# Four graph layers on one core: the self edge taken out of the gather lists, its row loaded plainly, nine chunks of edges per tile instead of ten

## What is computed

```python
# layer 0: 4 heads, slope 0.2
Wh = h @ W ; e = leaky_relu(s_i[:, None] + s_j[None, :]) ; mask by adj ; alpha = softmax(e)
out = elu(alpha @ Wh)
# layer 1: 1 head, slope 0.01:   out = h @ W + softmax(e) @ h
# layer 2: 4 heads, slope 0.2, biases: out = softmax(e) @ (h @ W + b)
# layer 3: 4 heads: q, k, v = h @ Wq + bq, ... ; out = softmax(q k^T / 8 + mask) @ v
```

## Time and profile before

| | |
|---|---|
| median of 3 runs | 2135.06 us (2132.64 to 2135.48) |
| profiled execution, its own time | 2136.06 us |
| its span, first to last instruction | 2134.3 us |
| busy: PE / DVE / ACT / POOL | 1360.3 / 1511.9 / 828.1 / 1288.1 us |
| mean granted TensorE clock | 0.851 |
| gathers | 1280 indirect DMAs on POOL |

### The profile page before, as it was taken

One profiled execution on the slowest core, in us unless ns is written; L12 is line 12 of the kernel. 1 busy time (PEld: TensorE's weight loads), 2 busy tenths in 40 slices (PEclk: granted clock), 3 DMA queues, 4 the chain that ended last, 5 costly groups with the idle time before them and its releaser, 6 DMA issues.

```text
span 2134.3 us, 24746 instructions
## 1 busy us (share of the span) xinstructions
PE 1360.3 (64%) x8038; PEld 1000.1 (47%) x8038; DVE 1511.9 (71%) x3362; ACT 828.1 (39%) x1804; POOL 1288.1 (60%) x1300
## 2 busy tenths in 40 slices
PE   3565322777667526666677447777778567777775
PEld 2434221555555414454455235555555355555554
DVE  2768897888777635555557357777777389999997
ACT  5777352677655501222222102322223223333332
POOL 0000067777777167777776277777773477777771
PEclk9999999778777858877878668998989689888998
DMA  9998134444444134444444244454543577777772
GB/s 357 387 382 304 14 81 117 112 124 115 117 117 118 35 102 107 113 114 112 115 115 104 61 106 129 138 140 136 140 139 98 162 225 228 228 226 226 226 225 63
DMA packets 151094, 328.57 MB, mean 154 GB/s; under 512 B 31275, under 2 KB 62897, under 8 KB 150961
## 3 DMA queue, kind: packets, MB, share of 16 engines
q0 software_dynamic: 71680, 213.24, 36.9%
q1 hardware_dynamic: 61584, 92.57, 12.3%
q10 hardware_dynamic: 17696, 21.12, 2.9%
HBM read 294.93 MB, written 31.90 MB: 153 GB/s over the span
## 4 chain that ended last, share of the span: by engine, by line
POOL 56%; issue 20%; PE 7%; DVE 7%; ACT 5%; DMA 3%; SPq 1%; ACTq 0%; POOLq 0%; DVEq 0%
POOL s_gb L785 56%; PE ps L1814 3%; PE ps L1736 3%; ACT s_a L816 2%; DMA s_adj<-in_adj_dram 2%; DMA s_gb<-s_tab,s_ji 1%; DVE s_gb L1537 1%; DVE s_F L1473 1%; DVE s_F L1471 1%; SPq L634 1%; ACT s_tb L934 1%; DVE s_ST L1359 0%; ACT s_hb L857 0%; DMA s_tab<-s_tb 0%; ACT s_S L971 0%
## 5 line engine op out<-in xcount | busy, mean ns | idle before, releaser
L785 POOL DMA_INDIRECT s_gb<-s_tab,s_ji x1280 | 1283.7, 1003 | 551.8 <-issue 388.1
L1814 PE MATMUL ps<-s_gb,s_S 128*128 128x260 f32 (+1 forms) x2048 | 574.9, 443 | 28.5 <-DVE s_gb L1537 25.2
L1814 PEld LDWEIGHTS ps<-s_gb,s_S 128*128 128x128 f32 x2048 | 453.3, 227 | 117.7 <-DVE s_gb L1537 29.9
L1537 DVE TENSOR_TENSOR s_gb<-s_gb,ps 128x1024 f32<-128x1024 f32 (+1 forms) x288 | 284.8, 1031 | 0.1
L1736 PE MATMUL ps<-s_wx,s_hT 128*128 128x264 f32 (+2 forms) x512 | 221.8, 569 | 86.9 <-ACT s_tb L932 48.4
L1787 PE MATMUL ps<-s_ident,s_sc 128*16 128x128 f32 (+3 forms) x408 | 78.4, 347 | 289.5 <-DVE s_sc L1432 284.3
L1427 DVE TENSOR_TENSOR s_sc<-s_sc,s_gb 128x80 f32<-128x80 f32 (+3 forms) x51 | 11.5, 226 | 287.9 <-DMA s_gb<-s_tab,s_ji 286.2
L971 ACT ACTIVATE s_S<-s_count,s_ji 128x128 f32<-128x128 f32 x512 | 156.5, 397 | 145.6 <-PE ps L1814 129.7
L1787 PEld LDWEIGHTS ps<-s_ident,s_sc 128*16 128x16 f32 (+3 forms) x408 | 39.3, 104 | 313.5 <-DVE s_sc L1432 292.9
L1776 PE MATMUL ps<-s_qs,s_ST 128*128 128x256 bf16 x960 | 153.5, 329 | 45.5 <-DVE s_tmp L1454 31.0
L1736 PEld LDWEIGHTS ps<-s_wx,s_hT 128*128 128x128 f32 x512 | 111.6, 241 | 147.8 <-ACT s_tb L932 55.2
(11 more groups left out here) (201 smaller groups left out, 2026.7 us busy)
## 6 DMA issues: line engine op xcount, KB each, us to landing
s_adj<-in_adj_dram SPq DMA_DIRECT2D x32, 2048.0 KB, 17.0
s_gb<-s_tab,s_ji POOLq DMA_INDIRECT x1280, 3.2
s_tab<-s_tb ACTq DMA_DIRECT2D x32, 256.0 KB, 4.1
s_tab<-s_tb ACTq DMA_DIRECT2D x31, 260.0 KB, 3.9
s_qs<-s_q SPq DMA_DIRECT2D x32, 192.0 KB, 3.9
s_q<-s_qs SPq DMA_DIRECT2D x15, 384.0 KB, 2.9
...
```

Source lines behind the costliest of these rows:

```text
L785: e.indirect_dma_start(gb[:, 0, k, :], None, self.tab_d[L.n], bass.IndirectOffsetOnAxis(ap=self.idx[:, t, k:k + 1], axis=0)).then_inc(self ...
L1537: e.tensor_tensor(vv[:, k0:k1], vv[:, k0:k1], wide(p[:, k0:k1, :], 3, L.hd), ALU.mult).then_inc(self.weighed)
L1814: m = e.matmul(o, S[:, i, :], g4[:, 0, k, lo:lo + o.shape[1]], start=(k == 0), stop=(k == KT - 1))
```

## The change

The edge of a node to itself is taken out of the lists, so that nine chunks hold the edges of a tile. The node's own row comes by a plain load, 128 rows at a time, into `mine`. The own edge's score `z` is worked out per node when the table is made (`vec_si` for layers 0 to 2, `vec_z` for layer 3), spread over the edges with the target's score, enters the maximum, and its weight goes through the sum as extra columns; `vec_finish` adds own weight times own row. Besides, the subtraction of the maximum moves: `vec_shift` ends with the backward scan, PE turns the maxima back, and DVE subtracts them from the scores in four small instructions (`vec_less`), before which ACT's exponential can't start. Layer 1 multiplies its rows as the others do. In `vec_step`, `vec_less` stands behind the second finish, in `vec_last_step` at the end.

```diff
-KT = 10
+KT = 9
@@ sp_own, called for tiles 0 to 3 at a layer's start, then for the tiles of group n+2 at the end of step n @@
+    def sp_own(self, e, L, t):
+        g = T * L.n + t
+        if g >= 4:
+            e.wait_ge(self.evac, g - 3)
+        a = D if L.n == 3 else 0
+        self.sp_dma(e, self.mine[:, t % 4, :], self.tab_d[L.n][P * t:P * t + P, a:a + D], self.own_in[t % 4])
@@ gp_layer @@
             if L.n == 3:
                 e.wait_ge(self.q_proj, T)
+                e.wait_ge(self.zed, 17)
@@ act_exp @@
+        e.wait_ge(self.lessened, G + 1)
...
+        e.activation(self.p_bank(L, n), sc[:, :, :, 0:H], ACT.Exp).then_inc(self.p_ok)
+        for t in tiles:
+            m = e.activation(self.rows(L, t)[:, 0, :, self.pcols(L, 2)], sc[:, :, t - tiles[0], :], ACT.Exp)
@@ vec_si @@
+        e.tensor_tensor(z, tb[:, :, D:D + H], tb[:, :, D + H:D + 2 * H], ALU.add).then_inc(self.v)
+        e.wait_ge(self.v, vs.up())
+        e.scalar_tensor_tensor(z, z, L.slope, z, ALU.mult, ALU.max).then_inc(self.v)
@@ vec_z, called by vec_r before its own instruction @@
+        e.tensor_tensor(prod, self.bank(0, D * a, D * c).rearrange("p (j d) -> p j d", d=D), k, ALU.mult).then_inc(self.zed)
+        e.wait_ge(self.zed, m + 1)
+        e.tensor_reduce(z, prod.rearrange("p j (h d) -> p j h d", h=4), AX, ALU.add).then_inc(self.v)
+        e.wait_ge(self.v, vs.up())
+        e.tensor_scalar(z, z, 0.125, None, ALU.mult).then_inc(self.v)
+        e.wait_ge(self.v, vs.up())
+        self.vec_split(e, z, r, [self.si3[:, t0:t0 + c, n, 0:4] for n in range(3)], self.si_ok)   # 4 small instructions
@@ vec_scores (now in layer 3 too, in place of act_double) @@
+            e.scalar_tensor_tensor(flat, flat, L.slope, flat, ALU.mult, ALU.max).then_inc(self.v)
...
-            m = e.scalar_tensor_tensor(twice[:, :, s, :], raw[:, 4 * s:4 * s + HC, :], L.slope,
-                                       raw[:, 4 * s:4 * s + HC, :], ALU.mult, ALU.max)
+            m = e.tensor_tensor(twice[:, :, s], raw[:, 3 * s:3 * s + HC], z[:, 3 * s:3 * s + HC], ALU.max)
         m.then_inc(self.raw_ok)
+        e.tensor_tensor(z, z, first, ALU.add).then_inc(self.v)
@@ vec_shift @@
-        e.tensor_tensor(F, pc, F, ALU.subtract).then_inc(self.shifted)
+    def vec_less(self, e, L, n):
+        e.wait_ge(self.back, G + 1)
+        e.wait_ge(self.v, vs.n)
+        for a in (0, H):
+            for s, k0, k1 in ((0, 0, 5), (1, 5, KT)):
+                to = sc[:, k0:k1, :, a:a + H]
+                m = e.tensor_tensor(to, to, pt[:, k0 - 3 * s:k1 - 3 * s, s], ALU.subtract)
+        m.then_inc(self.lessened)
@@ vec_weigh: three products of three chunks a tile, in layer 1 too @@
+            k = slice(3 * u, 3 * u + 3)
+            if L.n in (1, 2):
                 self.vec_onehot(e, L, 3 * (T * L.n + t) + u)
+            e.tensor_tensor(vv[:, k], vv[:, k], wide(p[:, k, :], 3, L.hd), ALU.mult).then_inc(self.weighed)
@@ vec_finish @@
-        e.reciprocal(rc, op).then_inc(self.v)
+        e.tensor_scalar(q, oq, self.alone[:, t:t + 1], None, ALU.add).then_inc(self.v)
+        e.wait_ge(self.v, vs.up())
+        e.tensor_tensor(rc, op, q, ALU.add).then_inc(self.v)
+        e.wait_ge(self.own_in[t % 4], 16 * (8 * L.n + t // 4 + 1))
+        e.tensor_tensor(by_head(mine), by_head(mine), wide(q, 2, L.hd), ALU.mult).then_inc(self.v)
+        e.reciprocal(rc, rc).then_inc(self.v)
+        e.tensor_tensor(ov, ov, mine, ALU.add).then_inc(self.v)
@@ vec_last_step @@
         self.vec_spread(e, L, n)
         self.vec_dots(e, 2 * n + 3)
+        self.vec_scores(e, L, n + 1)
         self.vec_finish(e, L, 2 * n)
         self.vec_finish(e, L, 2 * n + 1)
         self.vec_shift(e, L, n + 1)
         self.vec_dots(e, 2 * n + 4)
+        self.vec_less(e, L, n + 1)
```

More of the change, by code:

```diff
@@ L475, in __init__ @@
         self.turned_raw, self.shifted, self.back, self.p_ok = sem("traw"), sem("shifted"), sem("back"), sem("p")
-        self.ones_ok, self.weighed, self.apart, self.S_ok, self.agg = (sem(n) for n in ("one", "wei", "apart", "S", "agg"))
+        self.lessened, self.weighed, self.apart, self.S_ok, self.agg = (sem(n) for n in ("less", "wei", "apart", "S", "agg"))
         self.evac, self.x_new, self.ex_in, self.ex_out = sem("evac"), sem("x_new"), sem("ex_in"), sem("ex_out")
         self.missed_ok, self.met_sum, self.sym_ok, self.sym = sem("missed"), sem("met"), sem("sym_ok"), sem("sym")
-        self.ruler = sem("ruler")
+        self.ruler, self.zed, self.own_in = sem("ruler"), sem("zed"), [sem(f"own{n}") for n in range(4)]
         self.out = sem("out")
@@ L561, in rows @@
     def rows(self, L, t, n=1):
-        size = KT * L.row
+        size = KT * L.slot
         at = (0 if L.n == 3 else LOW) + t % L.ring * size
@@ L716, in sp_layer @@
                     self.sp_q_load(e, t)
+            for m in {0: (14, 15), 1: (15, 16), 2: (15, 16), 3: (30, 31)}[L.n]:
+                e.wait_ge(self.tab_out[m % 2], self.stored(L.n, m))
+            for t in range(4):
+                self.sp_own(e, L, t)
         for n in range(lo, hi):
@@ L726, in sp_layer @@
                 self.sp_q_store(e, n - 2)
+            for t in self.tiles(n + 2) if n < 15 else ():
+                self.sp_own(e, L, t)
         if hi == 17:
@@ L914, in act_rows @@
                     e.wait_ge(self.tab_out[t % 2], self.stored(3, t - 2))
+                    e.wait_ge(self.zed, self.group(t - 2) + 1)
                 else:
@@ L961, in act_onehot @@
         g = T * L.n + t
[L962 to L964 removed]
+        if g == 0:
             e.wait_ge(self.listed, 8)
@@ L968, in act_onehot @@
         for U in range(3 * g, 3 * g + 3):
-            many, k0 = self.many(U)
-            for i in range(many):
-                m = e.activation(self.s_part(U)[:, i, :], self.count[:], ACT.Square,
-                                 bias=self.irel[:, t, k0 + i:k0 + i + 1], scale=-1.0)
+            for i in range(3):
+                k = 3 * (U % 3) + i
+                m = e.activation(self.s_part(U)[:, i, :], self.count[:], ACT.Square, bias=self.irel[:, t, k:k + 1], scale=-1.0)
             m.then_inc(self.apart)
@@ L1169, in vec_norm, with vec_split @@
                                ALU.mult).then_inc(self.normed)
[L1171 to L1179 removed]
+    def vec_split(self, e, src, r, si, last):
+        vs = self.vs
         e.tensor_copy(si[0], src).then_inc(self.v)
@@ L1185, in vec_si @@
         e.wait_ge(self.v, vs.up())
+        e.tensor_tensor(si[2], r, si[1], ALU.subtract).then_inc(last)
+    def vec_si(self, e, l, m):
+        L, vs = LAYERS[l], self.vs
+        tiles = (2 * m, 2 * m + 1) if l == 0 else self.tiles(m)
+        H, a, c, t0 = L.heads, tiles[0] % 4, len(tiles), tiles[0]
+        tb = self.tbt[:, a:a + c, :]
+        z = tb[:, :, D + 2 * H:D + 3 * H]
+        r = self.sr[:, 0:2 * c * H].rearrange("p (j h) -> p j h", j=c)
+        e.wait_ge(self.tabbed, T * l + tiles[-1] + 1)
+        e.tensor_tensor(z, tb[:, :, D:D + H], tb[:, :, D + H:D + 2 * H], ALU.add).then_inc(self.v)
+        e.wait_ge(self.v, vs.up())
+        e.scalar_tensor_tensor(z, z, L.slope, z, ALU.mult, ALU.max).then_inc(self.v)
+        e.wait_ge(self.v, vs.up())
         if l == 1:
@@ L1194, in vec_r @@
         e.wait_ge(self.q0_ok, m + 1)
+        self.vec_z(e, m)
         e.scalar_tensor_tensor(self.qr[:, a:b], self.bank(0, D * a, D * (b - a)).rearrange("p (j d) -> p j d", d=D), 0.125,
@@ L1594, in vec_layer @@
                 self.vec_dots(e, 2)
+            self.vec_less(e, L, 0)
         for n in range(lo, hi):
@@ L1772, in pe_expand_q @@
             e.wait_ge(self.q_mul, x - 2)
-        for i in range(2):
+        for i in range(2 if c < 4 else 1):
             for s in range(3):
@@ L1811, in pe_add @@
             e.wait_ge(self.evac, g - 1)
-        for i in range(many):
-            k = k0 + i
-            m = e.matmul(o, S[:, i, :], g4[:, 0, k, lo:lo + o.shape[1]], start=(k == 0), stop=(k == KT - 1))
+        for i in range(3):
+            k = 3 * u + i
+            m = e.matmul(o, S[:, i, :], g4[:, 0, k, lo:lo + D + 2 * L.heads], start=(k == 0), stop=(k == KT - 1))
         if u == 2:
```

320 lines of the change are left out of this document (151 added, 169 removed).

## The result

The changed kernel takes 2067.99 us (median; 2065.19 to 2072.77) beside 2135.27 for the kernel before on the same chip: ratio 0.969, 95% interval 0.967 to 0.971, 67 us less where 76 were forecast. The profiled span went from 2134.3 to 2067.8 us. A second measurement of the same two kernels gave 0.970 (0.969 to 0.972).

What follows compares the result with a forecast made beforehand. Gathers on POOL were taken to bound layers 1 and 2, DVE layer 0, and DVE as much as POOL layer 3. Gains of 14.5 + 31 + 25.5 + 5.5 = 76.5 us gave 2059 us, range 2034 to 2100.

Steps and rivals of the forecast that it cites:

- POOL's step, 23.6 us: All layers: with two gathers fewer, POOL's step of two tiles falls from 26.2 to 23.6 us.
- Layer 0, 14.5: Layer 0: DVE stays the bound with steps of 22.0 us and earlier first weights; gain 14.5 us, bounds 19 to -4.
- The 2.5 us for the tail: Layer 0's end: two single tiles with longer finishes and z add 2.5 us.
- Layer 1, 31: Layer 1: POOL stays the bound until tile 29's wait, 37.5 us earlier, less a longer tail; gain 31, bounds 27 to 35.
- The tail's 6.7: Layer 1, from tile 29's wait to the next layer's first gather: added DVE work costs 6.7 us.
- the port's term: Layers 1 and 2: new DVE instructions with two SBUF inputs hold up POOL's gathers; 3 us taken, between 3 and 40.
- Layer 2, 25.5: Layer 2: DVE's step of 22.4 us stays under POOL's 23.6; 37.5 us earlier, less 12 behind; gain 25.5.
- `vec_z` ahead of the first gather, +5.2: End of layer 2: layer 3's gathers wait for the last `vec_z` product, making their start 5.2 us later.
- Layer 3, 5.5: Layer 3: steps save 2 us, first three tiles land 3.75 earlier, end unchanged; gain 5.5, bounds 14 to -17.
- A step near 26.2 with the smaller wait for PE kept: Layer 3: DVE work of 25.65 us plus the kept 0.55 wait for PE gives 26.2, against 26.29 before.
- the slower rival: Layer 3, SP's queue: q loads behind own-row loads come late; 5.1 us a step cancels all gain; chance 0.07.
- Rival of handovers (0.20): DVE's handovers are not hidden: steps of 23 in layer 0, 24 in layer 2, 27.3 in layer 3; 2098 us; chance 0.20.

Runs made afterwards that it cites:

- h2_layers: Changed kernel, own product and addition left out in layers 0 and 3, tenth gather added in layer 1, ninth left out in layer 2: 2080.64 us.
- h1_all: Changed kernel with subtraction before the last dots, layer 3's end reordered, layer 2's own-score sums behind the bank's release: 2049.95 us, 0.960 of the kernel before.
- e6: Changed kernel with the end of layer 3 in another order on PE and DVE, engines stopping during gathers: 2581.7 us, 0.940 of the kernel before.
- e8: Changed kernel with the same three edits as h1_all, engines stopping during gathers: 2578.4 us, 0.937 of the kernel before.
- f1: The kernel of e8 measured once more, engines again stopping during gathers: 2535.6 us, 0.948 of the kernel before.
- g0_changed: The changed kernel itself with nothing edited, measured and traced again without engine stops: 2068.91 us, 0.970 of the kernel before.

## Why the prediction was nearly right

It had the sign, the sum to 9 us of 76, and the picture: gathers in layers 1 and 2, DVE in layers 0 and 3. That the sum came so near is in part luck: layer 0 gave 5.3 us more than forecast, the other three 14.5 us less. By its steps:

- **POOL's step, 23.6 us.** 23.5 measured (375.8 us for 288 gathers in layer 1). The tenth gather put back in layer 1 costs 37.2 us (h2_layers) beside the forecast's 37.5 for taking it out. Shown.
- **Layer 0, 14.5; measured 19.8.** Right mechanism, terms mis-sized. The first weights came at 363.27 and not 365. From there to the last-but-one weights it took 330.2 us, the 330 of the forecast (a step of 22.0 in the mean). The 2.5 us for the tail were not there: from these weights to layer 1's first gather it is 41.9 us for 42.5. The rest is the 0.8 us by which the layer starts later. That DVE's list decides the layer is shown by h2_layers only in part: 0.52 us less a tile, 16.6 us in all, gave 10.8, as DVE then waits for ACT in many steps.
- **Layer 1, 31; measured 26.** The tail's 6.7 was 7.2. The 37.5 up to the last wait was 33.2, as the gathers left are longer: up to tile 29's last one they take 1.001 us each for 0.981, which is 15.1 us in all over the bare 0.945 each where it was 10.8. That is the port's term, to which I had given 3 us for layers 1 and 2 together; it came to 4.3 in layer 1 and 1.6 in layer 2. In the trace of layer 1 one gather a step is long and lies on the backward scan, as before; in ten of the fifteen steps it lies on the own product behind it too, and seven more gathers are longer by 0.2 us beside the own product and the addition to `x`. That the own products cause it fits this, but in no run without stops were they left out of layer 1.
- **Layer 2, 25.5; measured 21.3.** 36.1 for 37.5 up to the last wait, 14.8 for 12 behind it. A DVE step of 22.4 "just under 23.6" was 22.9 to 23.3 (h2_layers). The stated danger (DVE the bound, 0 to 12 us lost) was nearer than I put it: the wait for rows left is 0.58 us and not 1. In the end behind the last wait for rows, DVE's waits are 24.3 us in all for 23.3: 3.6 us for PE's turn back are new, which the forecast lacked, and the waits for PE's sums fell from 11.2 to 4.8 while those for ACT's q grew. So nearly all of the 14.8 us is more work on DVE, priced too low by about 2. The forecast's own +5.2 for `vec_z` also adds up to 4.9 only (1675.7 + 2.2 + 0.7 - 1673.67).
- **`vec_z` ahead of the first gather, +5.2.** The place is right (releaser of the first gather), the single-tile z took 1.8 and not 2.2, and moving its sums behind the release gives 0.7 a group. Over the end of layer 2 it is 2.7 us (h1_all); the two traces of the changed kernel differ by 0.9 in that stretch (85.0 and 84.1).
- **Layer 3, 5.5; measured 0.2.** This is the step that failed, by its last term: "the end (two groups) has longer finishes against a turn that no longer waits for ACT: 0". It was 8.2 us longer. The steps did better than forecast: 26.05 us in the mean, and the first one 4.3 shorter. What stood in the place of the 0 is the new wait of DVE for PE's turn back, 3.79 and 4.69 us, against 2.19 for the turn, which went as forecast, and 1.25 for a sum. PE's order had been laid out for a consumer that wasn't DVE, and the dots of tile 31, moved behind the scans, held PE up ahead of the turn back. e6, e8, f1 and h1 take 12 to 13.4 us from the stretch behind scan 15 by order alone. From the scan of group 14 to the end it was 53.1 us before the change, 61.2 after it and 48.7 in h1_all. I had costed `vec_less` as instructions and as a wait of its successor for ACT (0.35 forecast, 0.30 measured), and hadn't asked what it waits for itself.
- **A step near 26.2 with the smaller wait for PE kept.** Right in sum, but by the mix of two kinds that the forecast didn't know: mostly 25.5 us at a granted clock of 0.93, in which DVE's list decides, and 26.45 at 0.81, in which PE does. How many there are of each differs between traces of one kernel.
- **SP's queue.** The own loads went out at 1873.37, q 3.3 us later; PE never waited for q in a step. The order that the slower rival feared is there, and the slack sufficed.
- **Rival of handovers (0.20).** Part of it came, in the ends and not in the steps: 8.5 us of waits for the turn back in layer 3's end, 3.6 in layer 2's, where other waits shrank by nearly as much. The one in layer 2 was not tried away.

Open: what part of layer 3's long steps is PE's order and what its clock; why layer 0 has two kinds of steps too, 21.7 and 22.6 us, at nearly the same granted clock (0.76 and 0.77 in g0_changed), the longer ones with a wait of 0.9 us for PE's sums; and whether the own loads cost anything.
